# A fused four-adapter residual kernel: the last chunk ends with the experts' block, two ring slots swap their tenants, and tile 1's adapter rows are loaded first

## What is computed

```python
x = x + L0(x, language_ids, W, Wr, A, B)     # base + 2 * gated experts
x = x + einsum('bct,bcd->bdt', x, weights[condition])
x = x + einsum('bnr,bor->bno', einsum('bni,bri->bnr', x, B[id]), A[id])
x = x + (einsum('bti,oi->bto', x, W) + b) + 2.0 * lora(x, A[id], B[id])
```

## Time and profile before

| | |
|---|---|
| median of 3 runs | 934.01 us (933.2 to 934.93) |
| profiled execution | 928.95 us, of which 927.2 us are the span in the trace |
| mean granted clock of TensorE | 0.988 |
| moved from and to HBM | 187.71 MB, mean 202 GB/s |

### The profile page before, as it was taken

How to read it: one execution, slowest core, us unless ns; L and a number is a source line. 1 busy time by engine, 2 the same in 40 slices (tenths; PEclk the granted TensorE clock), 3 DMA queues, 4 the chain that set the end, 5 groups by cost and what they waited for, 6 DMA issues and landing times.

```text
span 927.2 us, 14846 instructions
## 1 busy us (share of the span) xinstructions
PE 903.1 (97%) x4788; PEld 802.5 (87%) x4788; DVE 545.7 (59%) x1421; ACT 348.2 (38%) x800; POOL 232.3 (25%) x349
## 2 busy tenths in 40 slices
PE   9999999999999997999999999999999999999994
PEld 7888888888888886899999999899998999999983
DVE  6655444453467326667667667567567567568652
ACT  5544333333344222343443443433433433433421
POOL 1010110010010013531531532532522522522500
PEclk9999999999999998999999999999999999999996
DMA  7988676998654653656766756656765766666624
GB/s 256 305 268 266 218 256 215 314 328 232 193 171 127 182 172 108 188 174 195 216 175 186 226 176 190 212 180 184 216 187 174 214 190 181 215 188 182 210 78 152
DMA packets 105312, 187.71 MB, mean 202 GB/s; under 512 B 15890, under 2 KB 66451, under 8 KB 105235
## 3 DMA queue, kind: packets, MB, share of 16 engines
q1 hardware_dynamic: 105234, 186.76, 65.9%
HBM read 143.20 MB, written 49.81 MB: 208 GB/s over the span
## 4 chain that ended last, share of the span: by engine, by line
PE 91%; DMA 3%; SPq 2%; issue 1%; DVE 1%; ACT 1%; POOL 0%; POOLq 0%; DVEq 0%
PE ps_o L1223 26%; PE ps_d L1249 17%; PE ps_w L1257 13%; PE ps_d L1257 9%; PE ps_s L1223 9%; PE ps_o L1271 5%; PE ps_d L1264 4%; PE ps_o L1278 3%; DMA mdraw<-t 2%; PE ps_s L1284 1%; PE ps_w L1264 1%; SPq L424 1%; DMA stat_raw<-stat 1%; SPq L452 0%; PE ps_s L1304 0%
## 5 line engine op out<-in xcount | busy, mean ns | idle before, releaser
L911 DVE TENSOR_TENSOR stat_lo<-stat_raw,stat_hi 128x1024 fp32r<-128x1024 f32 (+1 forms) x127 | 143.2, 1128 | 32.0 <-ACT stat_hi L692 22.6
L692 ACT ACTIVATE stat_hi<-stat_raw 128x1024 fp32r<-128x1024 f32 (+1 forms) x127 | 116.8, 933 | 14.1 <-POOL stat_raw L596 7.6
L1249 PE MATMUL ps_d<-w_hi,stat_hi 128*128 128x512 f32 x256 | 106.7, 417 | 4.7 <-POOL w_lo L621 4.7
L1249 PE MATMUL ps_d<-w_lo,stat_hi 128*128 128x512 f32 x256 | 101.5, 397 | 0.0
L1249 PE MATMUL ps_d<-w_hi,stat_lo 128*128 128x512 f32 x256 | 101.5, 396 | 0.0
L1223 PE MATMUL ps_o<-chunk_a_hi,stat_hi 128*128 128x512 f32 x216 | 84.6, 392 | 0.8 <-DVE chunk_a_lo L911 0.5
L1223 PE MATMUL ps_o<-chunk_a_hi,stat_lo 128*128 128x512 f32 x216 | 84.2, 390 | 0.0
L1223 PE MATMUL ps_o<-chunk_a_lo,stat_hi 128*128 128x512 f32 x216 | 84.1, 390 | 0.0
L621 POOL CAST w_hi<-mdraw 128x512 fp32r<-128x512 f32 x32 | 19.9, 621 | 217.7 <-DMA mdraw<-t 217.7
L596 POOL TENSOR_TENSOR stat_raw<-stat_raw,ident 128x128 f32<-128x128 f32 x40 | 22.7, 569 | 185.3 <-DMA stat_raw<-stat 185.3
L1249 PEld LDWEIGHTS ps_d<-w_hi,stat_hi 128*128 128x128 f32 x256 | 48.7, 190 | 15.3 <-issue 4.8
(11 more groups left out here) (206 smaller groups left out, 2265.8 us busy)
## 6 DMA issues: line engine op xcount, KB each, us to landing
up<-tu SPq DMA_DIRECT2D x128, 256.0 KB, 4.0
stat_raw<-stat SPq DMA_DIRECT2D x59, 512.0 KB, 4.3
mdraw<-t SPq DMA_DIRECT2D x128, 208.0 KB, 2.9
stat_raw<-x SPq DMA_DIRECT2D x32, 512.0 KB, 3.5
out<-outb SPq DMA_DIRECT2D x31, 512.0 KB, 5.4
t<-md_a SPq DMA_DIRECT2D x16, 576.0 KB, 6.2
rows_raw<-x SPq DMA_DIRECT2D x32, 256.0 KB, 3.4
chunk_a_raw<-mov SPq DMA_DIRECT2D x24, 256.0 KB, 5.5
```

The source lines that it names most:

```text
L692: return nc.scalar.activation(dst, src, ACT.Copy)
L911: return nc.vector.tensor_tensor(out=dst, in0=src, in1=rounded.bitcast(F32), op=ALU.subtract)
L1249: last = nc.tensor.matmul(plain_bank(t)[:, 0:WCOLS], rows[a][:, k, :], w[c][:, k, :], start=k == 0 and m == 0, stop=k == KB - 1 and m == l ...
```

## The change

The experts' block becomes the last group (60) and the U2 blocks of chunk 4 move one group forward; `M_DONE` becomes the last M0 group itself (51). Slot 3 (group 59's) now gets u2s, d3m and the bias row, slot 0 (group 60's) S[0] and S[1]. Reading the indices is taken out of load_md into `choose`. Behind the groups, SP now issues: ids of tile 1, s3, the last U2 stores, load_md(1), the mix, s2, s4, the bias; load_md(1) is gone from step 0. ScalarE does x0, u2s and d3m of tile 0 and x1 once group 59 is done, before it evicts group 60. In step 0 the product of S[0] and T1 is done in two halves, with the transpose of tile 1's hg between them.

```diff
-    GROUPS += [(4, s) for s in M0_BY_TWO + [B0_BLOCK] + U2_BLOCKS]
+    GROUPS += [(4, s) for s in M0_BY_TWO + U2_BLOCKS + [B0_BLOCK]]
-    M_DONE = LAST[4] - len(U2_BLOCKS)
+    M_DONE = FIRST[4] + len(M0_BLOCKS) - 1
-    X0_AT, X1_AT, S12_AT, OWN_AT = [(G - 4 + n) % RING for n in range(4)]
+    X0_AT, X1_AT, OWN_AT, S12_AT = [(G - 4 + n) % RING for n in range(4)]
@@ sync
+            def choose(t):
+                chosen2[t], chosen3[t] = index(AD2, t, NE2), index(AD3, t, NE3)
+
             def load_md(t):
-                chosen2[t], chosen3[t] = index(AD2, t, NE2), index(AD3, t, NE3)
@@ load_s2
                 if at(j, 0):
-                    sp.wait_ge(pe_group, G - 1)
+                    sp.wait_ge(pe_group, G)
@@ the loop over g
+                    choose(0)
                     load_md(0)
...
-                if g == G - 1:
-                    load_s2(0)
@@ behind the loop over g
+            choose(1)
+            load_s3(0)
             store_u2(G - 2)
+            load_md(1)
             sp.wait_ge(pool_const, CONSTS)
             load_mix(0)
-            store_u2(G - 1)
-            load_s3(0)
+            load_s2(0)
             load_s4(0)
-            sp.wait_ge(pe_group, G)
+            sp.wait_ge(pe_group, G - 1)
             sp.dma_start(bias_row[:, :], ...)
@@ step
-                if front:
+                if front and not at(j, 0):
+                    choose(b)
                     load_md(b)
...
+                    choose(a + 2)
                     load_md(a + 2)
@@ gpsimd, sums
                 if at(j, 0):
-                    pool.wait_ge(pe_group, G - 1)
+                    pool.wait_ge(pe_group, G)
@@ scalar
-                if g == G - 1:
-                    x0_hi(0)
...
+            x0_hi(0)
+
+            act.wait_ge(pe_group, G - 1)
+            ud_hi(0)
+            x1_hi(0)
             group_hi(G - 1)
-            ud_hi(0)
@@ scalar, step
                 if front:
-                    x1_hi(j)
+                    if not at(j, 0):
+                        x1_hi(j)
                     s_hi(j)
@@ tensor
-            def winograd(ps, rows, weights, first):
-                for k in range(HALF_KB):
+            def winograd(ps, rows, weights, first, ks=range(HALF_KB)):
+                for k in ks:
@@ tensor, step
-                    winograd(plain_bank(a), S[0], T1, True).then_inc(pe_p[4], 1)
+                    if back:
+                        winograd(plain_bank(a), S[0], T1, True).then_inc(pe_p[4], 1)
+                    else:
+                        winograd(plain_bank(a), S[0], T1, True, range(0, 2))
                     pe.wait_ge(dve_udb, b + 1)
                     gated_rows(b)
+                    if not back:
+                        winograd(plain_bank(a), S[0], T1, True, range(2, HALF_KB)).then_inc(pe_p[4], 1)
```

## The result

The changed kernel took 924.7 us (median of 4, 922.7 to 925.07) against 934.47 of the kernel before beside it (4 executions, 933.2 to 939.52), a ratio of 0.9881 with a 95% interval of 0.9842 to 0.992. Two later comparisons with many more executions of before gave 0.9905 (0.9882 to 0.9928) and 0.9914 (0.9883 to 0.9944). The profiled execution took 925.07 us, of which 923.3 are its span. So the kernel is faster by 8 to 11 us; the forecast was 8.1, with 924.0 to 930.5 us as its range. The traces say where the time went: at the point that was forecast. But the two spans differ by 3.9 us only.

The account below looks back on a forecast made before the run. TensorE, busy 97% of the span, was taken as the bound; 5.9 + 1.5 + 0.7 = 8.1 us off the 927.2 span gives 919.1, and off the 934.01 median 925.9 us, range 924.0 to 930.5.

Parts of the forecast that it names:

- Parts 1 to 3: Entry to the tile loop: mdraw loads earlier, x quarters behind them, POOL's casts; tile 1's plain product starts 5.9 us earlier.
- before SP asks: At load_md(1): ScalarE's copies and POOL's subtraction make pool_ud ready at 337.9, with the loads issued from 338.3.
- Part 4: TensorE's half clock behind the waits before tile 1's plain product: a 0.8 us stall leaves full clock, 1.5 us won.
- Part 5: Other waits around tile 1's plain product: vparts' 1.7 us goes, inside the 5.9; udb is ready 0.4 us in time.
- rival B: udb becomes the wait: TensorE stops inside tile 1's plain product for up to 1 us, time 926.9; chance 0.06.
- Part 6: Step 0's split product of S[0] and T1 covers the transpose of hg: the 0.7 us hgTb wait goes.
- Part 7: Order of the groups, load_md(0) and the experts' block's eviction before the tile loop: counted at nothing.
- low end: Whole kernel: s2 and s4 land in 2.8, the stall is gone, 8.9 off, plus the runs' spread of 0.9: 924.0.
- A: Before tile 1's plain product: x quarters come later behind mdraw and mix; gain 4.9 to 6.4, 927.6 to 929.1; chance 0.26.
- C: SP's queue: load_md(1) held until about 347 delays s2 and s4, making the kernel slower, 936; chance 0.04.
- D: Start of tile 1's plain product: another wait hidden by mdraw's stands there, so the change does nothing; chance 0.04.

Follow-up runs that it names:

- b_fill: Kernel before with twelve small identity matmuls behind repeated(0), in the place of TensorE's wait for tile 1's w columns; ratio 0.9995 to before.
- a_b0mid: Kernel of a_mixlast with the experts' block back in the middle, U2 last, and SP's order adapted; ratio 0.9931 to the kernel before.
- a_mdlast: Changed kernel with tile 1's ids and load_md(1) back behind s2, s4 and the bias; ratio 0.994 to the kernel before.
- a_mixlast: Changed kernel with the mix loads moved behind s2 and s4; ratio 0.988 to the kernel before.
- b_queue: Kernel before with SP's order alone changed: tile 1's ids and load_md(1) ahead of s3, s4 and the mix; ratio 0.9975 to before.
- b_fill2: Kernel before with 10 matmuls of 356 columns in front of repeated(0) and 28 behind it, in both waits; ratio 0.9982 to before.

## Where the prediction was right, and the step that was wrong

- **Parts 1 to 3** (5.9 us): 11.28 - 5.23 = 6.05. The walk through SP's queue held within 0.5 us at each row. load_md(1) went 0.4 us later, because pool_ud came at 340.06 (GpSimd's first subtraction took 1.48 us beside VectorE's x0 part, where I had 0.74). So "before SP asks" was wrong: SP waited there, and the delay went on to s2, issued 0.36 us late. Nothing hid it; it was made good by a landing of 3.2 us where I had taken 3.6, which is luck. What was late next was s2, as said.
- **Part 4** (1.5 us): 1.2 to 1.5 from plain(1) to hidden product 1, by 10.13 and 10.42 against 8.94; b_fill gives 1.4 to 1.7 for the clock alone. That a wait of up to 1.68 us leaves the clock alone does not follow from the earlier trace rows: the fall can come later than the window that I read. In a_b0mid it came after 355, 2 us behind the end of a wait of 2.00 and 1 us behind one of 0.89; a_mdlast lost the clock behind 1.85 us alone. So the fall in the trace of before, after 352, may belong to its wait of 1.68 too. With 0.6 it did not matter.
- **Part 5**: vparts is gone as a wait. udb came at 354.94, 0.06 us after TensorE was ready for it (354.88): the next matmul starts 0.35 and not 0.23 behind its predecessor at 354.65. So rival B was real and cost 0.1 us. Counted from the exponential's start (351.34), udb ended 3.60 us later and not 3.2. The two operations gsel of the gate made this difference, before and after:

```profile
353.26 0.48 DVE L1054 TENSOR_SCALAR gsel<-iota_e,topf,gw 128x8 f32<-128x8 f32 x2
...
352.45 0.92 DVE L1062 TENSOR_SCALAR gsel<-iota_e,topf,gw 128x8 f32<-128x8 f32 x2
```

In the trace of before GpSimd stood idle beside them; in the changed kernel it made tile 1's subtractions (to 353.34). In a_mdlast, where GpSimd was idle there again, they took 0.49.
- **Part 6** (0.7): 0.94.
- **Part 7** (nothing): as a cost, right. But the forecast put the gain of the whole change down to SP's order, and there it was wrong. One way to divide the 9.2 us of a_mixlast is: b_queue's order alone 0.7; the split 0.95; from b_queue to a_b0mid 2.7 (37.81 - 0.95 - 34.19), which holds the slots, ScalarE's new order and the places of load_md(1) and s2 in the queue; from a_b0mid to a_mixlast 4.85, the order of the groups with what it does to the queue, of which 1.55 is the half clock. Each step rests on one trace and depends on the others, and another sequence of steps would divide them otherwise. The sum was right because it was walked through with all of them in.
- **The sum and the range.** 8.1 us for the transition, 8.18 measured. The step that failed is the last one, from the profile to the time and to the low end: I took the 8.1 us off the median and widened the low end by "the runs' own spread of 0.9", which came from three executions. That term was mis-sized. Single executions of before lie between 928.3 and 936.1 us on one chip (23 of them) and between 932.1 and 941.9 on another (29), and the first comparison's own interval is 3.6 us to either side. With four executions of each kernel, one of them at 939.52, it came out at 11.1 us (0.9881 of 934.01 is 922.9, below my 924.0). With 12 and 23 executions of before it is 8.0 and 8.9.
- **Rivals.** A's place was right: the x quarters did become the last to come, with a wait of 0.6 us; they took 3.2 and 3.4 us to land, not 4.9. C and D had nothing to them here.

What stays open: the means give 8.5 and 9.0 us where the traces give 8.2 to 8.4, and which part of it is clock that no trace caught. The four kernels measured beside the 29 executions of before (b_fill2, b_queue, a_mdlast, a_mixlast) all gained more in the means than in the traces, by 0.9 to 3.0 us. Five of those 29 took 938 to 942 us, as did one of four in the first comparison, and none of the 35 on the other chip. No trace shows an execution of before that took 935 us or more, so why they are slow is not known, nor whether the changed kernel avoids it.

## What to carry to other kernels

When a load is late, list everything between it and its buffer's last reader, not only the queue: here a new order of the queue alone was worth 0.7 us in the trace, while the last group still had to be stored out of a buffer that the next loads needed. Walk the changed queue issue by issue with measured durations, and go on until you know what is late next. And take the spread of the metric from many executions, and compare stages between landmarks: two spans differed by 3.9 us where the change was worth 8.2.

## What the hardware showed that was not expected

VectorE's smallest operations ended with GpSimd's long ones, so not only GpSimd is slowed when the two run together. Beside the third and fourth sum of the changed kernel (348.04 to 350.77 above), VectorE's list shows:

```profile
348.18 0.17 DVE L1043 TENSOR_TENSOR lg<-ps_d,rbias 128x8 f32<-128x8 f32 x1
348.38 0.17 DVE L1045 MAX8 top<-lg 128x8 f32<-128x8 f32 x1
348.59 0.75 DVE L1047 TENSOR_TENSOR gdiff<-top 128x1 f32<-128x1 f32 x1
...
349.52 1.27 DVE L1050 CAST topf<-topi 128x2 f32<-128x2 uint32 x1
```

gdiff takes 0.16 us elsewhere and topf 0.17. Here the first ended at 349.34 and the second at 350.79, each within 0.03 us of the end of a sum that ran beside it (349.32, 350.77). In a_mixlast vparts took 1.10 us beside the fourth sum and ended at 348.56 (the sum: 348.52). It is so in the trace of before as well: the vparts of its 1.68 us wait took 0.72 us, to 351.45, beside a sum that ended at 351.41; in a_mdlast and in the changed kernel the same operation took 0.18 and 0.19. Not all operations are held: lg and the maximum ran in their usual 0.17 beside the third sum.

TensorE's clock fell to 1.2 GHz while the engine was busy, if it had been idle shortly before: in b_fill in the middle of 4.4 us of small matmuls, in a_b0mid 1.4 us into the plain product behind waits of 2.00 and 0.89 us (1.00 at 354 to 355, 0.50 at 356 to 357). In b_fill2, with matmuls of 356 columns in both places and 1.12 us of idling left, it stayed at 2.4 GHz. b_fill had left the first wait (1.80 us) empty, so whether the kind of matmul or the filling of that wait made the difference is not shown.
